# Attention chain, stages 0 to 2: units in fours, an order by planned times, and values in three shared banks

## The reference

```python
attn = softmax(einsum('bnd,bdm->bnm', q, k)); x = einsum('bcm,bnm->bcn', v, attn) + x            # stage 0
...
scores = einsum('bhqd,bhkd->bhqk', q, k) / sqrt(HD)                                          # stage 1, 16 heads
scores = scores * mask - 10000.0 * (1.0 - mask)
ctx = einsum('bhqk,bhkd->bhqd', softmax(scores), v);  x = x + ctx @ w_o + b_o
...
x = x + gelu(layernorm(x) @ w1 + b1) @ w2 + b2
...
attn = where(mask, einsum('bkhd,bnhd->bhkn', q, kmat) / DH, -inf)                             # stage 2
```

## Time and profile before

| | us |
|---|---|
| three timed runs: median (lowest to highest) | 2299.87 (2299.22 to 2300.43) |
| the profiled execution, its own time | 2294.0 |
| its span, first to last instruction | 2292.3 |
| TensorE busy in the span | 2094.7 (91%) |
| VectorE, ScalarE, GpSimd busy | 1292.5, 1168.0, 679.7 |

### The profile page before, as it was taken

How to read it: one execution, slowest core, us unless ns; L and a number is a source line. 1 busy time by engine, 2 the same in 40 slices (tenths; PEclk the granted TensorE clock), 3 DMA queues, 4 the chain that set the end, 5 groups by cost and what they waited for, 6 DMA issues and landing times.

```text
span 2292.3 us, 43483 instructions
## 1 busy us (share of the span) xinstructions
PE 2094.7 (91%) x14880; PEld 1799.8 (79%) x14880; DVE 1292.5 (56%) x4117; ACT 1168.0 (51%) x3854; POOL 679.7 (30%) x618
## 2 busy tenths in 40 slices
PE   5788999999999998986899999999799999999798
PEld 3566777777777776764799999998699999999687
DVE  3658675758576765333555555555555555555654
ACT  3556665756656565543444444444444444444432
POOL 2223333333333343221322222223222222123343
PEclk8999999999999999998899999999999999999989
DMA  6000000000000000000100000000000000000100
GB/s 240 3 1 11 1 11 1 10 1 11 1 6 6 1 4 2 3 1 24 36 24 14 23 23 23 18 23 22 8 24 23 18 23 14 23 23 14 37 14 23
DMA packets 23658, 45.19 MB, mean 20 GB/s; under 512 B 2400, under 2 KB 10080, under 8 KB 22624
## 3 DMA queue, kind: packets, MB, share of 16 engines
q1 hardware_dynamic: 21440, 32.62, 4.6%
q10 hardware_dynamic: 1440, 8.72, 1.0%
q0 software_dynamic: 640, 2.10, 0.3%
HBM read 41.33 MB, written 2.10 MB: 19 GB/s over the span
## 4 chain that ended last, share of the span: by engine, by line
issue 39%; POOL 8%; PE 3%; DVE 1%; POOLq 0%; DMA 0%; ACT 0%; SPq 0%; DVEq 0%; ACTq 0%
POOL probs L1220 2%; POOL w_qk L1196 2%; PE general L1730 2%; PE general L1574 1%; POOL w_o L1196 1%; POOL w_v L1196 1%; DVE oT L1556 1%; POOL X L1236 1%; POOL hT L1211 1%; POOL vrow L1200 1%; DMA raw_vrows<-vrows_dram 0%; PE general L1585 0%; DVE oT L1559 0%; DVE ctxT L1550 0%; POOLq L1195 0%
## 5 line engine op out<-in xcount | busy, mean ns | idle before, releaser
L431 POOL TENSOR_TENSOR probs<-probs,rsums 128x512 f32<-128x512 f32 (+1 forms) x288 | 283.4, 992 | 643.0 <-DVE rsums L632 641.9
L471 ACT ACTIVATE probs<-negated,negmax 128x128 f32<-128x128 f32 (+1 forms) x768 | 326.2, 429 | 66.3 <-DVE negmax L623 65.7
L1220 POOL TENSOR_TENSOR probs<-probs,rsums 128x512 f32<-128x512 f32 x128 | 133.2, 1041 | 764.3 <-DVE rsums L1418 764.3
L915 PE MATMUL pT_psum<-ident,probs 128*128 128x128 f32 x1088 | 177.3, 285 | 63.8 <-DVE probsT L638 39.1
L1327 ACT COPY probsT<-pT_psum 128x512 f32<-128x512 f32 x128 | 75.0, 586 | 288.3 <-PE pT_psum L1671 288.3
L915 PEld LDWEIGHTS pT_psum<-ident,probs 128*128 128x128 f32 x1088 | 128.2, 145 | 113.6 <-issue 84.9
L1574 PE MATMUL general<-hT,w_qk 128*128 128x512 f32 x768 | 207.0, 405 | 4.0 <-POOL hT L1211 4.0
L1574 PE MATMUL general<-w_o,oT 128*128 128x256 f32 x1536 | 194.8, 281 | 16.4 <-DVE oT L1425 16.4
L1574 PEld LDWEIGHTS general<-w_o,oT 128*128 128x128 f32 x1536 | 186.1, 188 | 24.6 <-DVE oT L1425 18.1
L1574 PE MATMUL general<-ctxT,w_qk 128*128 128x512 f32 x768 | 200.4, 397 | 0.0
L1319 ACT ACTIVATE probs<-scores,negmax 128x128 f32<-128x128 f32 x512 | 180.5, 370 | 29.8 <-DVE negmax L1410 29.7
(11 more groups left out here) (173 smaller groups left out, 4165.5 us busy)
## 6 DMA issues: line engine op xcount, KB each, us to landing
raw_qk<-w_qk_dram SPq DMA_DIRECT2D x34, 256.0 KB, 2.7
raw_v<-w_v_dram SPq DMA_DIRECT2D x17, 256.0 KB, 2.6
raw_vrows<-vrows_dram SPq DMA_DIRECT2D x17, 256.0 KB, 3.2
weights_a<-weights_a_dram ACTq DMA_DIRECT2D x2, 2048.0 KB, 18.2
raw_o<-w_o_dram SPq DMA_DIRECT2D x16, 256.0 KB, 2.6
weights_a<-weights_a_dram ACTq DMA_DIRECT2D x3, 1024.0 KB, 10.2
X<-x_dram SPq DMA_DIRECT2D x8, 256.0 KB, 7.4
ctx_in<-ctx_dram SPq DMA_DIRECT2D x8, 256.0 KB, 3.9
```

What stands on the lines that cost most here:

```text
L431: nc.gpsimd.tensor_tensor(pr, pr, rsums[:, n % 4, 0:segs].unsqueeze(2).broadcast_to([P, segs, width(kind) // segs]), ALU.mult).then_inc(s[ ...
L471: last = nc.scalar.activation(probs[:, n % PROBS, i * wide:(i + 1) * wide], src[:, i * wide:(i + 1) * wide], ACT.Exp, scale=1.0 if kind == ...
L915: last = nc.tensor.transpose(pT_psum[:, j * P:(j + 1) * P], probs[:, n % PROBS, j * P:(j + 1) * P], ident[:, :])
L1220: nc.gpsimd.tensor_tensor(pr, pr, rsums[:, t % 2, :].unsqueeze(2).broadcast_to([P, NB, P]), ALU.mult).then_inc(s["probs_ready"], 1)
```

## The change

The slots go. `SCORES`, `AFTER`, `WORK`, `NORMS`, `ADDS` and `MASKS` hold a planned time for each step of a group, in us from the group's origin; a group's origin is 100.0 after that of the one before (`PERIOD`). `AFTER` gives for each kind a distance from its block's scores and a distance between units. For each engine all steps are sorted by planned time into one list (`TENSOR_ORDER`, `VECTOR_ORDER`, `SCALAR_ORDER`, `GPSIMD_ORDER`, `LOAD_ORDER`), and the engine's loop runs through it. The numbers only set the order; nothing waits for a time. Of the tables the diff shows the first lines.

Self, cross and latent units go in blocks of four: `scores_of` writes the scores of four units alternately on four bands, and waits until all four score banks are free; `weigh_values` does so with the values of four, and waits for all four copies. Channel units stay in twos. `o_psum` goes: the values of a block become a use of the `general` banks, of which there are now three, handed out in the planned order of all uses. Semaphores `pv_done`, `o_copied` and `chan_done` are replaced by the banks' own. Since nothing else fixes the order of steps any more, copies, norms and gelus name what they must not overwrite (`wait_made`, `wait_scores`, `wait_values`). `mlp_down` waits for all four parts of its input, each part of an up projection for its norm.

```diff
-PERIOD = 18
-PAIRS_OF = {"chan": 2, "self": 4, "cross": 4, "lat": 8}
+PERIOD = 100.0
+UNITS_OF = {"chan": 4, "self": 8, "cross": 8, "lat": 16}
 BLOCK_UNITS = {"chan": 2, "self": 4, "cross": 4, "lat": 4}
...
-PAIR_SLOTS.update({("lat", p): 40 + p + (2 if p >= 4 else 0) for p in range(8)})
...
+SCORES = {('chan', 0): -58.87, ('chan', 2): -52.82, ('self', 0): -0.86, ('self', 4): 10.75, ('cross', 0): 77.91,
+          ('cross', 4): 89.86, ('lat', 0): 223.88, ('lat', 4): 234.24, ('lat', 8): 257.37, ('lat', 12): 270.89}
...
+AFTER = {'front': {'chan': (4.98, 0.38), 'self': (0.56, 2.99), 'cross': (3.75, 2.54), 'lat': (4.06, 1.55)},
+         'exps': {'chan': (5.05, 1.43), 'self': (6.75, 3.5), 'cross': (5.99, 2.94), 'lat': (11.68, 0.0)},
...
-NBANKS_A = 2
+NBANKS_A = 3
+VECTOR_READS = ("self_q", "cross_q", "lat_q", "self_o", "cross_o", "lat_o", "mlp1_down1", "mlp2_down1")
...
+FIRST_UNITS = [(kind, g, i * BLOCK_UNITS[kind]) for kind, g, i in BLOCKS_A]
+READ_AT = {name: at + (lag or 0.0) for name, (at, lag) in WORK.items()}
+TENSOR_ORDER = in_order([(SCORES[kind, u] + PERIOD * g, "scores", kind, g, u) for kind, g, u in FIRST_UNITS],
+                        of_units("turn", UNITS), of_units("values", FIRST_UNITS),
+                        of_names("work", WORK_ORDER, {name: at for name, (at, _) in WORK.items()}))
...
+USES_A = [(name[:-1] if "_down" in name else name, g) if step == "work" else (name, g, u // BLOCK_UNITS[name])
+          for step, name, g, u in TENSOR_ORDER if step == "values" or step == "work" and not name.endswith("_down1")]
...
-        o_psum = bank("o_psum")
         general = [bank(f"general{i}") for i in range(NBANKS_A)]
...
+                    wait_count(act, s["rsum_ready"], n - 3)
...
-                    wait_count(act, s["pv_done"], n - 3)
+                    wait_weighed(act, n - 4)
...
+                    earlier = before("read", [other for other in STREAM if STREAM[other] == STREAM[name]], name, g, SCALAR_ORDER)
+                    if earlier:
+
+                        wait_made(act, *max(((reader, earlier[1]) for reader in READERS[earlier[0]]), key=USES_A.index))
...
-                    dve.wait_ge(s["scores_ready"], n + 1 if kind == "chan" else n // 2 * 2 + 2)
+                    dve.wait_ge(s["scores_ready"], n + 1 if kind == "chan" else (n // 4 + 1) * 4)
...
+                for piece, kind, g, u in VECTOR_ORDER:
+                    if piece == "front":
+                        front(kind, g, u)
+                    elif piece == "rsum":
+                        rsum(kind, g, u)
...
-                def scores_of(kind, g, p):
-
-
-                    n = index(kind, g, 2 * p)
-                    wait_bank_read(n + 1)
-                    if p == 0:
+                def scores_of(kind, g, u):
+
+
+
+                    n = index(kind, g, u)
+                    if u == 0:
                         for name in {"lat": ("lat_q", "lat_k", "ctx_k")}.get(kind, (kind + "_q", kind + "_k")):
                             wait_copied(pe, name, g)
-                    c, b, r = unit_parts(kind, 2 * p)
+                    c, b, _ = unit_parts(kind, u)
                     if kind == "chan":
+                        wait_bank_read(n + 1)
                         for e in range(2):
                             nc.tensor.matmul(score_bank(n + e)[:, 0:D], q0T[:, b * D + e * P:b * D + (e + 1) * P], k0T[:, b * D:(b + 1) * D], start=True, stop=True).then_inc(s["scores_ready"], 1)
                         return
-                    segs = segments(kind)
-                    for j in range(segs):
-                        for e in range(2):
+                    wait_bank_read(n + 3)
+                    for j in range(segments(kind)):
+                        for e in range(4):
                             out = score_bank(n + e)
-                            band = slice(32 * (r + e), 32 * (r + e) + 32)
+                            band = slice(32 * e, 32 * e + 32)
                             if kind == "lat":
                                 last = nc.tensor.matmul(out[:, j * D:(j + 1) * D], qm[kind][band, c, j, b * P:(b + 1) * P], kT_lat[band, c, b, :, :], start=True, stop=True)
                             else:
                                 at = slice(j // 2 * P, (j // 2 + 1) * P)
                                 key = (kT_self if kind == "self" else kT_ctx)[band, c, at]
                                 last = nc.tensor.matmul(out[:, j * P:(j + 1) * P], qm[kind][band, c, j % 2, at], key, start=True, stop=True)
-                            if j == segs - 1:
-                                last.then_inc(s["scores_ready"], 1)
+                    last.then_inc(s["scores_ready"], 4)
...
-                def weigh_values(kind, g, p):
-
-
-                    n = index(kind, g, 2 * p)
-                    c, b, r = unit_parts(kind, 2 * p)
-                    for e in range(2):
+                def weigh_values(kind, g, u):
+
+
+
+                    units = BLOCK_UNITS[kind]
+                    n = index(kind, g, u)
+                    c, b, _ = unit_parts(kind, u)
+                    for e in range(units - 2, units):
                         wait_pT_copied(pe, n + e)
-                    i = block_of(kind, g, 2 * p)
-                    out = o_psum
-                    if 2 * p % BLOCK_UNITS[kind] == 0:
-                        wait_block_read(pe, i - 1)
-                    if p == 0:
+                    out, filled = wait_free(pe, kind, g, u // units)
+                    if u == 0:
                         for name in {"lat": ("lat_v", "ctx_v")}.get(kind, (kind + "_v",)):
                             wait_copied(pe, name, g)
                     if kind == "chan":
                         for e in range(2):
                             for m in range(2):
                                 last = nc.tensor.matmul(out[:, e * P:(e + 1) * P], v0T[:, b, m, :], probsT[:, (n + e) % 4, m * P:(m + 1) * P], start=(m == 0), stop=(m == 1))
-                            last.then_inc(s["pv_done"], 1)
+                        last.then_inc(filled, 1)
                         return
                     for j in range(4):
-                        for e in range(2):
-                            band = slice(32 * (r + e), 32 * (r + e) + 32)
+                        for e in range(4):
+                            band = slice(32 * e, 32 * e + 32)
                             pT = probsT[:, (n + e) % 4, j * P:(j + 1) * P]
-                            head = c * HPC + 2 * (r + e) + (j // 2 if kind == "lat" else j % 2)
+                            head = c * HPC + 2 * e + (j // 2 if kind == "lat" else j % 2)
                             columns = slice(32 * head, 32 * head + 32)
                             if kind == "lat":
                                 last = nc.tensor.matmul(out[band, 0:P], v_lat[:, j % 2, b, columns], pT, start=(j == 0), stop=(j == 3))
                             else:
                                 v = (v_self if kind == "self" else v_ctx)[:, j // 2, columns]
                                 last = nc.tensor.matmul(out[band, j // 2 * P:(j // 2 + 1) * P], v, pT, start=(j % 2 == 0), stop=(j % 2 == 1))
-                            if j == 3:
-                                last.then_inc(s["pv_done"], 1)
...
+                    last.then_inc(filled, 1)
...
+                for piece, kind, g, u in TENSOR_ORDER:
+                    if piece == "scores":
+                        scores_of(kind, g, u)
+                    elif piece == "turn":
+                        transpose_probs(kind, g, u)
```

More of the change, by code:

```diff
@@ new lines, with by_plan @@
+NORMS = {'ln1': -20.3, 'ln2': 54.61, 'ln3': 137.67, 'rms': 323.89}
+ADDS = {'self': 19.44, 'cross': 130.16, 'mlp1': 194.85, 'lat': 238.51, 'mlp2': 258.27}
+MASKS = {'cross': 50.55, 'lat': 161.35}
+def by_plan(times):
+    return sorted(((name, g) for name in times for g in range(GA)), key=lambda item: times[item[0]] + PERIOD * item[1])
+BLOCKS_A = [(kind, g, first // BLOCK_UNITS[kind]) for (kind, first), g in by_plan(SCORES)]
+UNITS = [(kind, g, i * BLOCK_UNITS[kind] + e) for kind, g, i in BLOCKS_A for e in range(BLOCK_UNITS[kind])]
@@ L153, in seed, with before @@
+LOAD_ORDER = in_order(of_names("ctx", [("chan_k", g) for g in range(2, GA)], {"chan_k": WORK["chan_k"][0] - 60.0}),
+                      of_names("mask", [("cross", g) for g in range(2, GA)] + [("lat", g) for g in range(1, GA)], MASKS))
+def before(step, names, name, g, order):
+    items = [(step_name, group) for kind_of_step, step_name, group, _ in order if kind_of_step == step and step_name in names]
+    at = items.index((name, g))
+    return items[at - 1] if at > 0 else None
 def seed(eng, sems):
@@ L861, in other_work @@
                     else:
[L862 to L863 removed]
+                        wait_copied(pe, {"self": "ln1", "cross": "ln2", "lat": "lat"}[name[:-2]], g)
                         if name.endswith("_v"):
```

296 lines of the change are left out of this document (135 added, 161 removed).

## The result

The changed kernel takes 2185.39 us (median; 2183.57 to 2186.75) beside 2300.15 (2299.22 to 2302.25) for the one before on the same chip: ratio 0.9499, interval 0.9483 to 0.9516. The forecast was 2195, range 2155 to 2245. Its profiled execution has a span of 2181.9 us against 2292.3.

What follows compares the result with a forecast made beforehand. TensorE, 94% busy in the steady stretch, was taken as the bound. Steady stretch 91, start 8 and end 6 us gave 105 us off, so 2195 us, range 2155 to 2245.

Steps and rivals of the forecast that it cites:

- The total: Whole kernel: 105 us off, from a steady period of 107.6 us instead of 123.4, to 2195 us.
- the start to 204 us: Before the steady stretch: 16 us come off TensorE's band work, about half of it counted, 8 us gained.
- the end: From 914 us on: half of 17 us of TensorE's latent attention work, less 3, so 6 us gained.
- Four units at once: Attention scores and values: four bands cost what two do, taking 16.6 us of TensorE's work off each period.
- The far bound of 1.65 us: Upper end for a four-band group, start to start; by it a period saves 7 us rather than 16.6.
- The same, so nothing: Values sharing three banks with projections: 7.7 us for each use before and after, so no cost or gain.
- Handovers "nothing": Score banks passing between four-unit blocks: no cost taken, with bounds of 0 to 1.5 us a block.
- rival 4: Slower: four-bank handover or turned buffers close a loop, no gain from 2 us a block, 2347 at 3; chance 0.06.
- The turns and the copies: TensorE's waits a period: 3.2 us for adjacent transposes of probabilities, 2.4 us left of waits for copies.
- rival 1: Order as tight as planned: TensorE idles 2 us, period 102.3, 130 to 140 us off, 2165 or less; chance 0.14.
- Rival 2: VectorE and its handovers as second bound: 0.7 us of waiting at each four-unit block, period 113.2, 2233 us; chance 0.13.
- Rival 3: Four bands run below rate, at the upper bound of a group's cost: period 117.2, 2257 us; chance 0.06.

Runs made afterwards that it cites:

- e1: Changed kernel, but each four-unit block's matmuls are written as two pairs, one behind the other; 2212.9 us.
- e3: Changed kernel, but the values have a bank of their own and the other work two, as before; 2222.3 us.
- e2: Kernel before, with its slots and banks, but scores and values of four units at once; 2306.7 us.
- e9: Changed kernel with GpSimd's three residual additions on X at other places of its queue; 2162.2 us.
- e6: Changed kernel with one more VectorE instruction, an unread multiplication of a constant tile, behind each reciprocal; 2204.2 us.
- e11: e9 plus, at each of the additions' three old places, one unused GpSimd addition that reads two SBUF tiles; 2172.0 us.
- e7: Changed kernel with pairs one behind the other and a bank of their own for the values, leaving the order alone; 2250.5 us.

## Why the prediction was right, and where it wasn't

**The total** was right, with luck in how it was spread. A period of 107.6 us was worked out, 105.8 came. Where the 114.5 us arose is read from the same step in both kernels, the down projections of the MLPs: those of the first group's MLP of stage 2 and of the sixth group's, before and then now:

```profile
339.97 3.72 PE L804 MATMUL general<-weights_a,upT 128*128 128x256 f32 x16
...
935.28 3.72 PE L804 MATMUL general<-weights_a,upT 128*128 128x256 f32 x16
```

```profile
331.72 3.62 PE L850 MATMUL general<-weights_a,upT 128*128 128x256 f32 x16
...
836.96 3.62 PE L850 MATMUL general<-weights_a,upT 128*128 128x256 f32 x16
```

In the first group's MLP of stage 1 nothing is gained (165.13 and 165.19), in the second's 3.9 us (262.34 and 258.47). So the start to 204 us gave at most 4 us, where 8 were worked out. At 339.97 it is 8.3 us and at 935.28 it is 98.3, 18.0 for each of the five groups between, where 15.8 were worked out. Start and steady stretch together were to give 99 by 914 us, so their errors nearly cancel. Behind 935.28 come another 16.2 us, where the end was to give 6. Part of the miss is also in the last step of the sum: 5.9 us were added from the profiled execution to the median, and for the changed kernel they are 1.8.

**Four units at once**: the price of a group was right on the choice between 1.09 and 1.65 us. Measured are 1.10, 1.08 and 1.01 us. The 16.6 us a period were 18.9. Part of the rest is probably that half as many groups also mean half as many changes between band groups and other work: the projection at 407.11 (L838), behind a band group, takes 1.83 us to the next start, and one of the same line at 411.55, behind a transpose, 1.72; 16 times 0.11 is 1.8 us, an estimate. The 1.3 times that would follow from "Part 3: Packing small matmuls" of the Trainium skill's "TensorE: Matmul & The Clock Gate" was not seen: a four costs 1.10 us where a pair costs 1.09. (0.3 of the 1.04 us of a pair is 0.31 us and not the 0.26 written there, which makes 5 us a period and 29 in all; the sum didn't use it.) What was wrong is where the gain was put. The far bound of 1.65 us, read from two adjacent pairs, is exactly what adjacent pairs cost in e1; but the prediction took it for self scores and values alike, and there values cost 1.47 and latent scores nothing more. Most of TensorE's saving comes already with pairs brought together by the order, and the interleaving is worth 28 to 32 us, not the 91 that hung on this step.

**"The same, so nothing"** for the banks of the values is the step that failed, although the total held. It divided the period by uses per bank, 7.7 us each before and after. An average says nothing of bursts: in the new order projections follow one another closely, and two banks make TensorE wait 5.1 us a period (e3). The sum came out because it compared the old order with its two banks and its 6.6 us of idle time with the new order and three. Had the change kept a bank of its own for the values, the argument would have given the same 2195, and 2222.3 came (e3).

**Handovers "nothing"** held in the changed kernel: no row has TensorE waiting for a front or for a block's read. It held because of the order. In the slot order TensorE's idle time rose by 12.3 us a period, 1.5 for each of eight blocks, most of it in the loop of rival 4; rival 4 had 2 us as the point from which nothing is gained, and start and end took the rest (e2). The prediction saw the mechanism but gave the order no price of its own.

**The turns and the copies**: 3.2 + 2.4 = 5.6 us of waits a period were worked out, 6.6 came. The four adjacent turns cost 3 x 0.77 + 0.55 = 2.9 us, close to the 3.2 worked out from the earlier trace rows; a fifth wait for ScalarE, of 0.33 us, makes 9.5/3 = 3.2. The copies by VectorE cost 3.4, and not because they were queued behind long work in general: 2.84 of it is one wait, from three maxima that GpSimd held up. The earlier trace rows had the sign of it: maxima of the self units have a mean of 380 ns there, while the undisturbed ones take 0.28 us; the prediction used the mean as the cost of a front and didn't ask why. The granted clock below 0.99, named as a cost not counted, came with the long wait (0.98), but the kernel before pays about as much at its own long wait.

**Rivals.** The tighter period (1) came only in e9: 101.6 us and 2162, beside 102.3 and at most 2165 in rival 1. The number agrees and the mechanism doesn't: rival 1 had 100.2 of work and 2 of idle time, e9 has 96.6 and 5.0, with the adjacent turns still in it. What kept the changed kernel from it is GpSimd beside the maxima, which neither side of rival 1 names. Rival 2 was right in part: a microsecond more on VectorE costs a third of one (e6), but no 0.7 us at each block was seen. Rival 3 fell with the first timeline. Rival 4 did not happen here and did in e2.

## What to carry to other kernels

Small matmuls on different bands overlap as soon as they stand next to each other; ask an order for that first, interleaving comes second and pays only where the blocks' handovers are spread. Count a shared buffer by who waits in a burst, never by the mean time for each use, and price a removed or added bank by the idle time of both kernels. When rows of one instruction spread four to one in length (0.28 and 1.35 us), look at what the neighbouring engine reads at that moment: moving three instructions a period of an engine that was 41% busy brought 19 us, where interleaving brought 32. Price a long wait of TensorE with what its clock does behind it.

## What the runs showed of the hardware

A VectorE instruction that reads two tiles in SBUF (`masked` and `madd_cross`) was held up by a GpSimd instruction that reads SBUF: it took 0.28 us alone and beside fills, 0.89 to 1.35 us beside additions and multiplications, and ended 0.1 to 0.2 us after GpSimd's. The latent maxima, whose scores are in PSUM, had a mean of 419 ns in the changed kernel, 417 with the additions moved beside them. This is what the Trainium skill's "SBUF — State Buffer", section "SBUF: two separate sides", states of the pair of ports that the two engines share, a lock held for a whole instruction and, for two inputs in SBUF, only against a GpSimd instruction that reads SBUF; the runs agree with both halves.

Two pairs of fp32 matmuls on different bands, one pair wholly behind the other in the order, overlap: 1.65 us for 32 rows of 128 columns where two separate pairs take 2.18, and 1.09 us for 16 rows of 256 columns, which is all that four interleaved take.

TensorE's granted clock fell to 0.50 behind single waits of 2.84 us (for 3.25 us, changed kernel) and 2.42 us (kernel before), stayed at 1.00 behind waits of 0.70 (e9) and 1.46 us (e11), and did both at 1.5 us (e7 and e1).
